# Four layers of cross attention and feed-forward: the softmax reciprocal of the three sixteen-head attentions moved from VectorE to ScalarE, with its correction on VectorE and Pool

## What is computed

```python
x = x + attention(_layernorm(x), ctx)      # layers 1, 2, 3
q, k, v = x @ Wq + bq, ctx @ Wk + bk, ctx @ Wv + bv   # then split into 16 heads
attn = softmax(scale * q @ k.T)            # 256 x 64 for each sequence and head
ctx = attn @ v                             # heads joined again
return ctx @ Wo + bo
```

## Time and profile before

| | |
|---|---|
| median of 3 runs | 1288.74 us (1287.62 to 1289.69) |
| the profiled execution | 1287.9 us; span in the profile 1286.1 us |
| busy share of the span | PE 80%, VectorE 73%, ScalarE 48%, Pool 28% |
| reciprocals (L718) | 48, from 281.2 us to 1038.9 us |
| ACT_TABLE_LOAD on ScalarE | 31, of 1.28 us each |

### The profile page before, as it was taken

How to read it: one execution, slowest core, us unless ns; L and a number is a source line. 1 busy time by engine, 2 the same in 40 slices (tenths; PEclk the granted TensorE clock), 3 DMA queues, 4 the chain that set the end, 5 groups by cost and what they waited for, 6 DMA issues and landing times.

```text
span 1286.1 us, 21270 instructions
## 1 busy us (share of the span) xinstructions
PE 1024.6 (80%) x7331; PEld 662.8 (52%) x7331; DVE 943.0 (73%) x2271; ACT 616.2 (48%) x958; POOL 361.8 (28%) x339
## 2 busy tenths in 40 slices
PE   5868500878969987996598888897879969999998
PEld 3653200844547753553166565576645446666665
DVE  4686699778866666777798889887468856666666
ACT  3424566366622336652565556664276523333332
POOL 5600000011200024451887788775002100000000
PEclk8889955989989999999599889998999979999999
DMA  7000000100000000000000000000000000000000
GB/s 261 1 1 1 1 0 0 59 4 2 2 2 1 0 1 1 2 1 1 1 1 1 1 0 0 0 0 1 1 2 2 2 1 9 9 8 8 8 9 17
DMA packets 8956, 13.47 MB, mean 10 GB/s; under 512 B 816, under 2 KB 6704, under 8 KB 8624
## 3 DMA queue, kind: packets, MB, share of 16 engines
q1 hardware_dynamic: 8880, 12.46, 2.8%
HBM read 10.36 MB, written 2.10 MB: 10 GB/s over the span
## 4 chain that ended last, share of the span: by engine, by line
PE 45%; DVE 34%; issue 12%; ACT 6%; POOL 2%; DVEq 1%; DMA 0%; SPq 0%; POOLq 0%; ACTq 0%
DVE big L718 6%; DVE big L713 6%; PE psum L1879 5%; PE psum L511 5%; PE psum L1882 5%; PE psum L1893 5%; PE psum L1574 3%; DVE big L1785 2%; PE psum L1366 2%; PE psum L1319 2%; DVE tmp L1750 2%; PE psum L1328 2%; ACT psum L1642 2%; PE psum L252 2%; DVE amax L1129 2%
## 5 line engine op out<-in xcount | busy, mean ns | idle before, releaser
L713 DVE TENSOR_REDUCE big<-psum 128x16 f32<-128x1024 f32 x96 | 114.4, 1221 | 70.9 <-PE psum L465 38.0
L1699 POOL TENSOR_TENSOR big<-big 128x512 f32<-128x512 f32 x128 | 134.7, 1086 | 19.9 <-ACT big L1622 19.9
L1929 ACT ACTIVATE big<-psum 128x512 f32<-128x512 f32 x80 | 47.8, 598 | 143.3 <-PE psum L1879 143.1
L1642 ACT ACTIVATE psum<-big,tmp 128x512 f32<-128x512 f32 x128 | 84.9, 687 | 37.2 <-DVE big L1785 33.3
L383 POOL TENSOR_TENSOR big<-big,w_const 128x256 f32<-128x256 f32 x48 | 34.7, 724 | 229.8 <-PE psum L511 216.0
L1785 DVE SCALAR_TENSOR_TENSOR big<-big,tmp,psum 128x512 f32<-128x512 f32 x128 | 90.3, 743 | 4.8 <-ACT psum L1642 1.8
L1709 POOL TENSOR_TENSOR big<-big 128x1024 f32<-128x1024 f32 x32 | 75.4, 2366 | 64.0 <-DVE big L1785 64.0
L1982 DVE TENSOR_TENSOR big<-big,psum 128x512 f32<-128x512 f32 x80 | 54.4, 687 | 53.1 <-PE psum L1882 52.9
L718 DVE RECIPROCAL big<-psum 128x256 f32<-128x256 f32 x48 | 83.9, 1749 | 11.8 <-PE psum L511 11.8
L1893 PEld LDWEIGHTS psum<-tmp,big 128*128 128x128 f32 x512 | 66.7, 191 | 40.0 <-issue 36.3
L619 ACT ACTIVATE big<-psum 128x1024 f32<-128x1024 f32 x64 | 62.0, 1021 | 51.3 <-PE psum L495 51.3
(11 more groups left out here) (239 smaller groups left out, 2391.2 us busy)
## 6 DMA issues: line engine op xcount, KB each, us to landing
out<-X SPq DMA_DIRECT2D x8, 256.0 KB, 2.3
tmp<-in_pack_f SPq DMA_DIRECT2D x1, 1924.0 KB, 7.8
w_f<-in_pack_f SPq DMA_DIRECT2D x1, 1280.0 KB, 12.3
tmp<-in_pack_once SPq DMA_DIRECT2D x1, 960.0 KB, 7.5
X<-in_x SPq DMA_DIRECT2D x1, 768.0 KB, 5.3
w_a<-in_pack_a SPq DMA_DIRECT2D x3, 256.0 KB, 7.6
w_a<-in_pack_a SPq DMA_DIRECT2D x1, 704.0 KB, 9.7
w_f<-in_pack_f SPq DMA_DIRECT2D x1, 576.0 KB, 5.0
```

What stands on the lines that cost most here:

```text
L713: dve.tensor_reduce(nm, psum[:, 1 + 2 * t:3 + 2 * t, :].rearrange("p c (r l k) -> p (c r) l k", r=2, k=SK), AX.X, ALU.max, negate=True).th ...
L1642: act.activation(bank(EX_BANK + h % 2), ssum[t][:, h * 512:(h + 1) * 512], ACT.Exp, bias=shift2[:, t * NH2 + h:t * NH2 + h + 1]).then_inc( ...
L1699: ins = pool.tensor_tensor(ssum[t][:, h * 512:(h + 1) * 512].rearrange("p (i j) -> p i j", i=ROWS2), st[:, 0, h, 0:ROWS2].unsqueeze(2).to_ ...
```

## The change

In `heads_dve` the reciprocal of bank 6's right half z is gone. ScalarE computes r = exp(-ln z) in two instructions (`recip`, last in its round, behind `take_turned`). VectorE computes e = z*r, then ov = (e - 2)*(left half of bank 6), and Pool computes oT = ov*r (`out`). That is one Newton step, r*(2 - z*r), with the sign turned round; the residual then subtracts instead of adding. PV(b, 0) now waits for `ov` of b-1, while O(b) still waits for `oT` of b, now Pool's. In Pool's list `out(b-1)` stands behind `weights(b+2)`. In a1 and a3 Pool's list is also written by sequence instead of by group.

```diff
--- before.py
+++ after.py
@@ -256,13 +256,13 @@
             act.wait_ge(sem(s, "turned"), at(s, "turned") + g + 1 + 2)
             act.activation(hT[:, j, :], bank(0), ACT.Copy).then_inc(sem(s, "hT"), 1)
 
-        def residual(dve, s, g, src, last_sub, ready):
+        def residual(dve, s, g, src, last_sub, ready, op=ALU.add):
 
             dve.wait_ge(*ready)
             if s in HAS_ROW:
                 dve.wait_ge(sem(s, "biased"), at(s, "biased") + g + 1)
             xg = X[:, ds(4 * g, 4), :]
-            dve.tensor_tensor(xg, xg, src.rearrange("p (t n) -> p t n", t=GT), ALU.add).then_inc(sem(s, "res"), 1)
+            dve.tensor_tensor(xg, xg, src.rearrange("p (t n) -> p t n", t=GT), op).then_inc(sem(s, "res"), 1)
             tail_stats(dve, s, g, last_sub)
 
         def tail_stats(dve, s, g, last_sub):
@@ -312,7 +312,8 @@
 
         HSUB = ("a1", "a2", "a3")
         PER = dict(k_ps=1, v_ps=4, k=8, kb=2, ka=2, v=4, zero=2, mask=0, kv=B, q_ps=B, qe=0, qT=B, q16=B, mx_ps=2 * B,
-                   mx=2 * B, nm_ps=B, nmT=B, st_ps=B, pt=2 * B, pv=B, rz=B, oT=B, o_ps=B, r=0, prep=0)
+                   mx=2 * B, nm_ps=B, nmT=B, st_ps=B, pt=2 * B, pv=B, lnz=B, rz=B, e=B, ov=B, oT=B, o_ps=B,
+                   r=0, prep=0)
         ATT_A0 = dict(k_ps=2, v_ps=4, k=4, kb=2, v=8, mask=8, q_ps=N_GROUPS, qT=N_GROUPS, q16=N_GROUPS, mx_ps=N_GROUPS,
                       mx=N_GROUPS, kv=N_GROUPS, st_ps=N_GROUPS, pt=N_GROUPS, pv=N_GROUPS, rz=N_GROUPS,
                       oT=N_GROUPS, o_ps=N_GROUPS)
@@ -345,7 +346,9 @@
                 self.nm = [a.take(256) for _ in range(2)]
                 self.nmT = [a.take(256, BF16) for _ in range(2)]
                 self.oT = [a.take(256) for _ in range(2)]
-                self.rz = a.take(256)
+                self.rz = [a.take(256) for _ in range(2)]
+                self.lnz, self.e = a.take(256), a.take(256)
+                self.ov = [a.take(256) for _ in range(2)]
                 if rope:
                     self.kT, self.t1, self.t2 = a.take(B * SK), a.take(512), a.take(512)
                     self.qe, self.qse = [a.take(256) for _ in range(2)], [a.take(256) for _ in range(2)]
@@ -394,6 +397,13 @@
                     pool.wait_ge(hs("st_ps"), hat(s, "st_ps") + b - L.ahead + 1)
                 pool.wait_ge(hs("r"), 2 * b + 2)
                 pool.tensor_tensor(L.qT[b % L.ahead], L.qe[b % 2], L.qse[b % 2], ALU.add).then_inc(hs("qT"), 1)
+
+            def out(b):
+
+                pool.wait_ge(hs("ov"), hat(s, "ov") + b + 1)
+                if b >= 2:
+                    pool.wait_ge(hs("o_ps"), hat(s, "o_ps") + b - 1)
+                pool.tensor_tensor(L.oT[b % 2], L.ov[b % 2], L.rz[b % 2], ALU.mult).then_inc(hs("oT"), 1)
 
             if L.rope:
                 rotate(0)
@@ -408,13 +418,22 @@
                         rotate(b + 4)
                     if b + 2 < B:
                         weights(b + 2)
+                    if b:
+                        out(b - 1)
                     if b % 2 and b // 2 + 1 < N_GROUPS:
                         rows(b // 2 + 1)
             else:
-                for g in range(N_GROUPS):
-                    weights(2 * g)
-                    weights(2 * g + 1)
-                    rows(g)
+                weights(0)
+                weights(1)
+                rows(0)
+                for b in range(B):
+                    if b + 2 < B:
+                        weights(b + 2)
+                    if b:
+                        out(b - 1)
+                    if b % 2 and b // 2 + 1 < N_GROUPS:
+                        rows(b // 2 + 1)
+            out(B - 1)
 
         def heads_pe(pe, L):
             s = L.s
@@ -503,7 +522,7 @@
                     if b == 0:
                         pe.wait_ge(hs("k"), hat(s, "k") + 8)
                     else:
-                        pe.wait_ge(hs("oT"), hat(s, "oT") + b)
+                        pe.wait_ge(hs("ov"), hat(s, "ov") + b)
                 for e in range(2):
                     for r in range(4):
                         w = W["vmask8"][:, 32 * e:32 * e + 32] if which else \
@@ -620,6 +639,17 @@
                                psum[:, 1 + 2 * half:3 + 2 * half, :].rearrange("p c n -> p (c n)"), ACT.Exp,
                                bias=L.kmT[:, b:b + 1] if L.keys else 0.0, scale=L.scale).then_inc(hs("pt"), 1)
 
+            def recip(b):
+
+                act.wait_ge(hs("pv"), hat(s, "pv") + b + 1)
+                if b:
+                    act.wait_ge(hs("rz"), hat(s, "rz") + b)
+                act.activation(L.lnz, bank(6)[:, 256:512], ACT.Ln).then_inc(hs("lnz"), 1)
+                act.wait_ge(hs("lnz"), hat(s, "lnz") + b + 1)
+                if b >= 2:
+                    act.wait_ge(hs("oT"), hat(s, "oT") + b - 1)
+                act.activation(L.rz[b % 2], L.lnz, ACT.Exp, scale=-1.0).then_inc(hs("rz"), 1)
+
             def norm_half(b):
 
                 g, hf = (b + L.ahead + 2) // 2, (b + L.ahead + 1) % 2 == 0
@@ -675,6 +705,9 @@
                 take_ahead(b)
                 if b == 2:
                     keys16(1)
+                if b:
+                    recip(b - 1)
+            recip(B - 1)
 
         def heads_dve(dve, L, nxt):
             s = L.s
@@ -714,15 +747,19 @@
                                   AX.X, ALU.max, negate=True).then_inc(hs("mx"), 1)
 
             def norm(b):
-                dve.wait_ge(hs("pv"), hat(s, "pv") + b + 1)
-                dve.reciprocal(L.rz, bank(6)[:, 256:512]).then_inc(hs("rz"), 1)
+
                 dve.wait_ge(hs("rz"), hat(s, "rz") + b + 1)
+                if b:
+                    dve.wait_ge(hs("ov"), hat(s, "ov") + b)
+                dve.tensor_tensor(L.e, bank(6)[:, 256:512], L.rz[b % 2], ALU.mult).then_inc(hs("e"), 1)
+                dve.wait_ge(hs("e"), hat(s, "e") + b + 1)
                 if b >= 2:
-                    dve.wait_ge(hs("o_ps"), hat(s, "o_ps") + b - 1)
-                dve.tensor_tensor(L.oT[b % 2], bank(6)[:, 0:256], L.rz, ALU.mult).then_inc(hs("oT"), 1)
+                    dve.wait_ge(hs("oT"), hat(s, "oT") + b - 1)
+                dve.scalar_tensor_tensor(out=L.ov[b % 2], in0=L.e, scalar=2.0, in1=bank(6)[:, 0:256],
+                                         op0=ALU.subtract, op1=ALU.mult).then_inc(hs("ov"), 1)
 
             def res(g):
-                residual(dve, s, g, bank(7), False, (hs("o_ps"), hat(s, "o_ps") + 2 * g + 2))
+                residual(dve, s, g, bank(7), False, (hs("o_ps"), hat(s, "o_ps") + 2 * g + 2), ALU.subtract)
 
             normalise(dve, s, 0, 0)
             if L.keys:
```

## The result

| | before | changed |
|---|---|---|
| median, lowest to highest | 1288.38 us, 1287.62 to 1289.69 (4 runs) | 1370.53 us, 1368.37 to 1371.25 (4 runs) |
| ratio | | 1.0634, 95% interval 1.0615 to 1.0652 |
| span in the profile | 1286.1 us | 1369.4 us |
| a1, first key matmul to last output matmul | 120.4 us | 151.9 us |
| a2, the same | 137.3 us | 163.7 us |

The forecast was 1367 us, range 1346 to 1396. The change costs 82 us. The three stages together are 83.2 us longer; the rest of the program takes 910 us in both profiles.

What follows compares the result with a forecast made beforehand. TensorE's own work was taken to bound the loops, with VectorE's reciprocal on the chain. Pool hold-ups and ScalarE's queue, less time given back, summed to 26.8 + 26.8 + 25.4 = +79 us on 1287.9: 1367 us, range 1346 to 1396.

Steps and rivals of the forecast that it cites:

- What bounds the kernel before: Loops of a1 and a2: TensorE's own work; shortening VectorE's reciprocal chain can save only PV's waits, 0.17 and 0.60 us.
- The hold-up on Pool: O waits on Pool for `weights`, then `out`: 1.82 us in each of 13 rounds a stage, 39 in all.
- A round without a turn: O moves by +1.82 us, MX gives back 0.39: net +1.43 us.
- A turn round: `recip` behind `take_turned` delays PV: +2.90 us, 1.82 from Pool and 1.08 from ScalarE's queue.
- The copy at b = 2: In a1 and a3, a 1.99 us copy ahead of `recip` on ScalarE: +0.9 us beyond the turn round.
- The sum: 26.8 us each for a1 and a3, 25.4 for a2: +79 us, giving 1367 us; chance 0.80.
- The clock: TensorE's clock inside the loops was taken as held despite new gaps, so nothing was added to the sum.
- The first rival: TensorE drops to 1.2 GHz inside the loops, some 6 stretches of 10 us: 24 us more, 1391 us; chance 0.11.
- The other rivals: Pool no hold-up, 1295 us, 0.03; faster, 1277 us, 0.04; a table load for each Ln and Exp, 0.02.
- The table loads: On ScalarE, Ln and Exp each need a 1.28 us table load: 96 more, over 120 us; chance 0.02.
- The faster rival: Only TensorE's wait in PV changes, neither T nor `weights` delaying: 10 to 11 us less, 1277 us; chance 0.04.
- What would show it: Profile signs: O waits for Pool 39 times, some 65 us; PV waits about 1.3 us in turn rounds alone.

Runs made afterwards that it cites:

- e1_out_first: Changed kernel with out(b-1) moved ahead of weights(b+2) in Pool's list: 1294.43 us, ratio 1.0055 to the kernel before.
- The fillers: Idle identity matmuls ahead of O's wait for oT: 6 on the changed kernel, 1358.56 us; 9 with Pool's product also written twice, 1390.08 us.
- e3_both: Changed kernel with out ahead of weights on Pool and recip ahead of take_turned on ScalarE: 1280.43 us, ratio 0.9940 to the kernel before.
- e6: Changed kernel with 6 idle identity matmuls ahead of O's wait for oT in the 39 held rounds: 1358.56 us, ratio 1.0543.
- e7: Changed kernel with Pool's product written twice and 9 idle matmuls ahead of O's wait for oT: 1390.08 us, ratio 1.0783.
- e4_pool_twice: Changed kernel with Pool's product written twice, the first into a spare buffer: 1422.85 us, ratio 1.1062 to the kernel before.

## Why the prediction was right

The time came out 3.5 us above the forecast, and the main term, the hold-up on Pool, is what was forecast. That it came so close is partly luck: the sum was too high by 9 us or more and left out a cost of 12 us or more, and the two nearly cancel.

- *What bounds the kernel before* was read rightly: PV's two waits, 0.17 and 0.60, are all that the shorter chain can give; with both lists mended the rounds of a1 got shorter by 0 and 0.39. The chain itself was forecast as 1.8 to 1.9 us; from the start of Ln at 317.02 to the end of `ov` at 318.35 + 0.42 it takes 1.75.
- *The hold-up on Pool* was right in place and number. Its size was forecast at 1.82 us, with the hand-over taken from VectorE's 0.15. Pool hands over in 0.05: from the start of `weights` at 317.13 to O at 318.60 are 1.47, where 1.57 was counted. That is 39 x 0.1 = 4 us too much.
- *A round without a turn* was forecast at +1.43 and measured 7.36 - 6.06 = +1.30; less the hand-over the two agree. The 0.39 given back by MX is there: MX waits for the exponential now in such rounds, and not for PV.
- *A turn round* was forecast at +2.90 and measured 8.73 - 6.10 = +2.63. Beside the hand-over, the logarithm overlaps the end of `take_turned` by 0.1 (it starts 0.49 after its start, not 0.60), and `ov` takes 0.42 and not 0.49. That is 14 x 0.17 = 2 us too much.
- *The copy at b = 2* was priced at 0.9 beside the turn round's 2.90. In a3 of e1_out_first, where the clock holds in that round, the copy adds 1.9 us to it, against 1.1 in the kernel before: 0.8. In the change the whole round costs 4.9 instead of 3.8, as the clock falls in it in both stages.
- *The sum* was thus too high for a held clock. The fillers give nearly that case by measurement: ratio 1.0543, 70 us above the kernel beside it, with the clock not quite back (25.0 us at the lower level, against 13.6). The sum said 79. The hand-over and the turn rounds are 6 of the 9 us; the rest was not traced.
- *The clock* was the step that failed. "The sum above takes it as held", on the strength of one window at a1's end. It was not held: 51.2 us at the lower level instead of 13.6, worth 12 us by the fillers, which gave back 26 of these 38 us. The sign that was named for a wrong prediction, PEclk at 0.5 inside the loops, did appear. The first rival had the mechanism, with 6 stretches of 10 us for 24 us; it happened at half that size, in more and shorter stretches. The window that spoke against it was also read too narrowly: 1.3 us behind its end the same trace has the clock at the lower level for 10 us (the row below this list). The Trainium skill ("TensorE: Matmul & The Clock Gate", the HAM clock gate) has it that the half clock is the default and that activity releases it. The runs agree: 51.2 us at the lower level with the waits open, 25.0 with them filled; 133.1 and 29.4 with the longer ones. The clock should have had a term in the sum.
- *The other rivals* are settled. Pool does hold O up, in the order of its list. The table loads did not come: L651 follows L647 by 0.41 us, and both profiles have 37 of them (31, as the table of the kernel before says, is a miscount). The faster rival, with its condition of neither `weights` nor T standing before the new steps, is what e3_both builds; it was priced at 10 to 11 us less, and it gives 0.6%, some 8 us.
- *What would show it*: O's wait was 69.9 us in 42 times (forecast 65 in 39; three more are the last of each stage); PV's wait in turn rounds was 1.12 by the profile (forecast 1.3), and 3.0 at b = 2 in a1 and a3.

The kernel before, right behind the window of the earlier trace rows (PEclk is the third number from the end):

```profile
373.40:383.40 10.00, 5.33 (x18) 4.00 (x19) 5.06 (x29) 3.36 (x7) 0.00 (x0) 0.50 0.00 1
```

What stays open is why the clock falls in one round and not in the next that looks alike. The one place where it nearly always falls is around the longest wait, the 3.0 us before PV at b = 2, in seven of eight cases (a1 and a3 of the change, e1, e6 and e7). The fillers stand elsewhere and don't fill that wait, so part of their 25.0 and 29.4 us lies there; behind the eighth (a3 of e1) the clock stays full.

## What to carry to other kernels

Where an engine takes its list in order, the place of a new step in it matters more than its length: ask of each step that somebody will wait for what the instruction ahead of it waits for. Here `weights` waited for PV(b, 1), and O, which stands right behind PV(b, 1) in TensorE's list, already wanted the result of `out`. Moving `out` up by one place was worth 76 us. All that the new arithmetic gave, once both places were right, was 8. Moving work off the busy engine pays no more than the wait that it ends, here 0.2 and 0.6 us a round, and may pay less if another wait takes its place: 0 and 0.4 were measured.

## What had not been expected of the hardware

- Waiting costs twice on TensorE. In e4_pool_twice a wait that grew by 29 us made the kernel 52 us slower, as TensorE's time at 1.2 GHz in the three stages rose from 51 to 133 us; the longest waits for Pool there were 2.7 us, and the longest before PV 3.0. Idle matmuls in those waits gave 33 us back.
- Pool hands its result over to TensorE in about 0.05 us (317.86 + 0.69 to 318.60), faster than VectorE in 0.15. The profile's spans on Pool are rough, so the 0.05 is less sure than the 1.47 us from the start of `weights` to O.
- The subtract-and-multiply of 256 columns with one operand in PSUM (scalar_tensor_tensor, 421 ns) costs VectorE no more than a plain product (425 ns), and a reciprocal of the same size four times as much (1749 ns).
